# The value products of two head pairs in one group, in every second slot, and the side work in another order

## The reference, cut to what matters

```
x: [16, 512, 128]                      # 16 batches, 512 tokens, 128 channels
x = x + 0.5 * ffn(layernorm(x))        # spiking FFN: relu(x Wfc^T)^2 Wproj^T, 5 steps of a membrane
x = x + attention(layernorm(x))        # 16 heads of 64, ALiBi slope * distance, causal, softmax
x = x + 0.5 * ffn(layernorm(x))        # the same FFN weights

attention(x):
  q, k, v = split(x @ w_qkv);  q *= 64 ** -0.5
  p   = softmax(causal(q k^T - slope_h * |i - j|))
  out = concat_h(p v) @ w_out + b_out
ffn(x): y = relu(x Wfc^T)^2 Wproj^T;  5 times: mem = 0.9 mem + y - (mem > 1);  result = mean of (mem > 1)
```

## Time and profile before

| what | value |
| --- | --- |
| device time, median of 3 runs | 1568.95 us (1568.69 to 1569.36) |
| the profiled execution's own time | 1571.02 us |
| its span in the trace | 1569.2 us |
| granted TensorE clock, mean | 0.998 of full speed |
| busy: PE, PEld | 99%, 80% |
| busy: DVE, ACT, POOL | 70%, 83%, 59% |
| DMA moved | 163.10 MB, mean 104 GB/s |

### The profile page before, as it was taken

The page is one execution under the profiler, slowest core; times in us unless marked ns, Lnnn a source line. Parts: engine busy times, 40 slices in busy tenths (PEclk is TensorE's granted clock), DMA queues, the critical chain, the costliest instruction groups (busy, mean ns, idle before and its releaser), DMA issues.

```text
span 1569.2 us, 33807 instructions
## 1 busy us (share of the span) xinstructions
PE 1547.5 (99%) x10399; PEld 1252.8 (80%) x10399; DVE 1102.2 (70%) x4091; ACT 1301.9 (83%) x3497; POOL 928.3 (59%) x1255
## 2 busy tenths in 40 slices
PE   8999999999999999999999999999999999999998
PEld 7778878887887888888788788878888878888776
DVE  6576776676776677776677766767776777766745
ACT  6888888888887888888888888888888888888884
POOL 4556656666665566556656566666655665566552
PEclk9999999999999999999999999999999999999999
DMA  4454454444455445444444544444554454444540
GB/s 119 91 115 105 98 121 99 105 107 101 107 111 113 98 92 118 108 105 105 104 109 98 121 99 103 107 102 105 111 115 98 94 120 104 102 105 102 114 103 20
DMA packets 80194, 163.10 MB, mean 104 GB/s; under 512 B 12816, under 2 KB 30864, under 8 KB 79888
## 3 DMA queue, kind: packets, MB, share of 16 engines
q1 hardware_dynamic: 80016, 160.94, 47.2%
HBM read 6.88 MB, written 4.19 MB: 7 GB/s over the span
## 4 chain that ended last, share of the span: by engine, by line
PE 96%; DVE 2%; ACT 1%; issue 1%; POOL 0%; POOLq 0%; DVEq 0%
PE bank L497 19%; PE bank L483 18%; PE bank L469 12%; PE bank L470 10%; PE bank L449 8%; PE bank L450 7%; PE bank L453 7%; PE bank L544 7%; PE bank L554 2%; PE bank L555 2%; PE bank L557 2%; PE bank L527 1%; ACT prob L1149 1%; PE bank L646 1%; PE bank L564 0%
## 5 line engine op out<-in xcount | busy, mean ns | idle before, releaser
L1350 POOL TENSOR_TENSOR prob<-prob,rsum 128x512 f32<-128x512 f32 (+3 forms) x1024 | 746.3, 742 | 583.7 <-DVE rsum L805 581.4
L1149 ACT ACTIVATE prob<-negsc,negmax 128x512 f32<-128x512 f32 (+3 forms) x1024 | 576.8, 566 | 164.6 <-DVE negmax L796 162.6
L796 DVE CUSTOM_DVE_ANT_0 negsc<-bank,dist 128x512 f32<-128x512 f32 (+3 forms) x1024 | 467.5, 475 | 0.3 <-issue 0.3
L805 DVE RECIPROCAL rsum<-sums 128x1 f32<-128x1 f32 (+1 forms) x768 | 123.4, 161 | 399.5 <-PE bank L470 382.4
L1162 ACT COPY probT<-bank 128x512 f32<-128x512 f32 x635 | 355.5, 587 | 46.4 <-PE bank L483 40.6
L483 PE MATMUL bank<-ident,prob 128*128 128x128 f32 x2540 | 356.1, 273 | 0.5 <-POOL prob L1350 0.3
L469 PE MATMUL bank<-keys,queries 128*128 128x256 f32 (+2 forms) x1024 | 350.3, 353 | 2.1 <-issue 2.0
L483 PEld LDWEIGHTS bank<-ident,prob 128*128 128x128 f32 x2540 | 299.1, 140 | 28.7 <-POOL prob L1350 5.6
L470 PE MATMUL bank<-keys,queries 128*128 128x256 f32 (+2 forms) x1024 | 319.7, 324 | 0.0
L497 PE MATMUL bank<-probT,vals 128*64 128x512 f32 x2032 | 301.5, 439 | 0.2 <-DVE queries L920 0.2
L497 PEld LDWEIGHTS bank<-probT,vals 128*64 128x64 f32 x2032 | 134.4, 136 | 159.6 <-issue 124.6
(11 more groups left out here) (143 smaller groups left out, 2190.1 us busy)
## 6 DMA issues: line engine op xcount, KB each, us to landing
queries<-queries SPq DMA_DIRECT2D x381, 256.0 KB, 2.9
keys<-k_lo SPq DMA_DIRECT2D x254, 128.0 KB, 2.4
keys<-keys SPq DMA_DIRECT2D x127, 128.0 KB, 2.3
x_in<-in_L_attn_x_dram SPq DMA_DIRECT2D x16, 256.0 KB, 3.1
out_dram<-x SPq DMA_DIRECT2D x15, 256.0 KB, 2.7
prob<-in_L_attn_w_qkv_dram SPq DMA_DIRECT2D x1, 1024.0 KB, 7.4
prob<-in_L_attn_w_qkv_dram SPq DMA_DIRECT2D x1, 512.0 KB, 8.2
probT<-in_L_attn_w_out_dram SPq DMA_DIRECT2D x1, 512.0 KB, 9.4
```

Source lines behind the costliest of these rows:

```text
L796: ins = dve.tensor_tensor_reduce(negsc[:, k % 3, col:col + WIDTH[i]], src, dist[:, N - WIDTH[i]:N], SLOPES[2 * p + h], MASKED, ALU.add, AL ...
L805: dve.reciprocal(rsum[:, p % 2, cols], sums[:, p % 2, cols]).then_inc(s_rsum, 1)
L1149: ins = act.activation(prob[:, p % 2, h, PCOL[i]:PCOL[i] + WIDTH[i]], negsc[:, k % 3, col:col + WIDTH[i]], ACT.Exp, bias=negmax[:, p % 2, ...
L1350: ins = pool.tensor_tensor(pr, pr, rsum[:, p % 2, seg:seg + 1].to_broadcast([P, WIDTH[i]]), ALU.mult)
```

## The change

1. The value products of two pairs stand directly behind one another, in slots 1, 3, 5 and 7, instead of those of one pair in every slot. A pair's value products come two or three slots behind its scores instead of two, so the ring `probT` grows from 10 to 20 places.
2. All tables of the side work and of the order within a beat are others: which beat each "q", "k", "v", "t", "fc", "y", turn, accumulate, membrane step and norm has. `SIDE` has 48 entries as before, of the same kinds. The values' index `i` now runs from 0 to 7 over the batch (`i // 2` is the pair of pairs).
3. In the tail, the statistics of the third norm are aggregated, inverted and used by halves: two tiles, then two tiles, where all four went together.

```diff
-TRING = 10
+TRING = 20
 TBEAT = [
-    [1, 2, 2, 5, 5],
+    [1, 1, 2, 3, 4],
...
-ACCBEAT = [7, 6, 8, 8, 11, 7, 11, 8]
-OUTEV = (2, 1)
+ACCBEAT = [5, 10, 6, 13, 7, 11, 8, 8]
+OUTEV = (2, 3)
...
 SIDE = [
-    (2, 0, "fc1", 3, 1), (2, 0, "q", 0, 0), (2, 1, "ot", 0, -1), (2, 2, "y1", 0, 1), (2, 2, "k", 0, 0),
-    (2, 3, "v", 0, 0), (2, 4, "pv", 0, 0), (2, 5, "y1", 1, 1),
...
+    (2, 0, "q", 0, 0), (2, 0, "fc1", 2, 1), (2, 2, "k", 0, 0), (2, 3, "v", 2, 0), (2, 4, "fc1", 3, 1),
+    (2, 4, "ot", 0, -1),
+    (3, 0, "v", 3, 0), (3, 0, "k", 0, 0), (3, 2, "q", 0, 0), (3, 3, "pv", 0, 0), (3, 3, "pv", 1, 0),
...
-SPIKE3 = [(6, 4), (7, 3), (8, 3), (8, 4), (9, 2), (9, 4)]
-LN1 = dict(stats=(0, 0), aggregate=(0, 2), rstd=(0, 3), normalise=(0, 4))
+SPIKE3 = [(7, 3), (8, 5), (9, 2), (9, 2), (9, 4), (9, 4)]
+LN1 = dict(stats=(0, 0), aggregate=(0, 1), rstd=(0, 2), normalise=(0, 2))
...
+        def pv_pair(b, s, i):
+
+            return before(b, s, 3 - i)
...
+        def acc_at(p):
+
+            return divmod((p - p % 2 + 3) * BEATS + ACCBEAT[p], BEATS)
...
                 elif kind == "pv":
                     for j in PVORDER:
-                        pv(bank or side_bank[n % 2], *before(b, s, 2), j)
+                        pv(bank or side_bank[n % 2], *pv_pair(b, s, i), j)
...
                         if part == "A":
-                            for back in (3, 2):
-                                if ACCBEAT[(s + 2 - back) % PAIRS] == k + BEATS * (back - 2) and exists(*before(b, s, back)):
-                                    accumulate(*before(b, s, back))
+                            for p in range(PAIRS):
+                                if acc_at(p) == (s, k):
+                                    accumulate(b, p)
+                                elif acc_at(p) == (s + PAIRS, k) and b > 0:
+                                    accumulate(b - 1, p)
...
                 for t in range(NT):
+                    if w == 3 and t == NT // 2:
+                        dve.wait_ge(s_rstd[3], B + 1)
...
                         ins = dve.bn_stats(stats[:, 2, t, :], x2[:, t, :])
-                ins.then_inc(s_stats[3], 1)
-                dve.wait_ge(s_stats[3], b + 1)
-                aggregate(3, b)
+                    ins.then_inc(s_stats[3], 1)
+                    dve.wait_ge(s_stats[3], B + half)
+                    for t in range(half * NT // 2, (half + 1) * NT // 2):
+                        ins = dve.bn_aggr(meanvar[:, 2, t, :], stats[:, 2, t, :])
+                    ins.then_inc(s_mv[3], 1)
...
-                bb, pp = before(b, p, 2)
+                bb, pp = before(b, p, TRING // len(TRUNS))
...
-                inverse_std(3, B - 1)
+                for half in range(2):
+                    tiles = TILE_HALVES[half]
+                    pool.wait_ge(s_mv[3], B + half)
+                    pool.tensor_tensor(vareps[:, 2, tiles], meanvar[:, 2, tiles, 1], eps[:, tiles], ALU.add).then_inc(s_ve[3], 1)
+                    pool.wait_ge(s_ve[3], B + half)
+                    pool.tensor_tensor(rstd[:, 2, tiles], vareps[:, 2, tiles], minus_half[:, tiles], ALU.pow).then_inc(s_rstd[3], 1)
```

More of the change, by code:

```diff
@@ L316, in freed @@
             if kind == "pv":
-                bb, pp = before(b, s, 2)
-                return s_attlo, pair_no(bb, pp)
+                return s_attlo, pair_no(*pv_pair(b, s, i))
             return s_x2, b + 1
@@ L324, in last_user @@
                 s, _, kind, i, off = SIDE[m]
-                if m % 2 == n % 2 and off in offsets and (kind != "pv" or exists(*before(b, s, 2))):
+                if m % 2 == n % 2 and off in offsets and (kind != "pv" or pv_exists(b, s, i)):
                     return freed(kind, i, b + off, s)
@@ L609, in slot @@
                             for n, kind, i, off, _ in side_at(s, k, offsets):
-                                if kind == "pv" and not exists(*before(b, s, 2)):
+                                if kind == "pv" and not pv_exists(b, s, i):
                                     continue
@@ L764, in tail @@
                     wait(pe, *last_user(len(SIDE) - (len(SIDE) - n) % 2, b, (-1, 0)))
-                for back in (3,):
-                    if ACCBEAT[PAIRS - 1] >= BEATS:
-                        accumulate(b, PAIRS - 3)
+                for p in range(PAIRS - 2):
+                    if acc_at(p) >= (PAIRS, 0):
+                        accumulate(b, p)
                 for j in PVORDER:
@@ L935, in low_half @@
                 elif kind == "pv":
-                    attention_low((bank or side_bank[n % 2]), *before(b, s, 2))
+                    attention_low((bank or side_bank[n % 2]), *pv_pair(b, s, i))
             def third_spikes(b, s, k):
@@ L1001, in slot @@
                     for n, kind, i, off, ss in side_at(s, k - 1, offsets):
-                        if kind == "pv" and not exists(*before(b, ss, 2)):
+                        if kind == "pv" and not pv_exists(b, ss, i):
                             continue
@@ L1218, in high_half @@
                     act.copy(ysb[:, i * 2 * C:(i + 1) * 2 * C], src[:, 0:2 * C]).then_inc(s_ysb[w], 1)
-                elif kind == "pv" and exists(*before(b, s, 2)):
-                    att_out((bank or side_bank[n % 2]), *before(b, s, 2))
+                elif kind == "pv" and pv_exists(b, s, i):
+                    att_out((bank or side_bank[n % 2]), *pv_pair(b, s, i))
             def slot(b, s, par, offsets):
```

68 lines of the change are left out of this document (35 added, 33 removed), and 21 rows, old and new, of the table SIDE.

## The result

The changed kernel takes 1578.84 us (median of 3 runs, 1576.63 to 1579.60) against 1568.95 before: ratio 1.0061, 95% interval 1.0047 to 1.0075. It is slower by 0.6%, where the forecast was 1549.0 us (1544 to 1557) and faster with 93%. The profiled execution took 1579.60 us with a span of 1577.8.

What follows compares the result with a forecast made beforehand. TensorE's own instruction list was taken as the bound. From the profiled 1571.02 us: -20.8 (twos) + 2 (keys) + 0 (start) - 1.0 (tail) = 1551.2; the median run is 2.07 less, so 1549 us, range 1544 to 1557.

Steps and rivals of the forecast that it cites:

- What bounds the kernel, and a switch's price: TensorE's own instruction list sets the time; entering and leaving a value group costs 0.33 us (0.31 to 0.36).
- The twos save 20.8 us: Value products of two pairs in one group: 63 entries and exits go, at 0.33 us each (19.5 to 22.7).
- Rival D: At the handover inside a doubled group the second pair pays the whole switch again: no gain, 1570 us; 3%.
- C: Rival: a weight load of 0.137 us shows at each handover between pairs, up to 8.6 us: 1558 us; 5%.
- The other tables: Reordered side work and beats: same work, priced at nothing; ScalarE's load was compared with PE's in the light slots.
- rival B: ScalarE sets the pace in light slots 0, 1 and 2, 0.7 us a batch: 1560 us; 8%.
- rival A: The keys come late for slot 3 in every batch, 2.5 us each, 40 us in all: 1587 us; 4%.
- PE's idle time in the loop grows by more than some 5 us: The sign, in the new trace's loop, by which the forecast would be wrong.
- The keys' way, 2 us: Key relay from slot 2's products to slot 3's scores: fits in the median, late landings cost 2 us (0 to 24).
- the margin of 0.3 us: Slot 2's key relay takes 4.8 us against PE's way of 5.1; it fails when a landing is late.
- Start, 0: Batch 0: an earlier first norm against ScalarE's pace in slots 1 and 2; bounds -4 and +3, taken as 0.
- Tail, -1.0: Last batch's third norm by halves: the first FFN products' input ready 1.0 us sooner (0.4 to 1.5).

Runs made afterwards that it cites:

- e13_mid: e10 with one 128-column full-weight product between the two halves of each doubled value group, 63 in all: 1590.79 us, ratio 1.0139.
- e14_ahead: e10 with the same 63 products of 128 columns ahead of the doubled value groups, not within them: 1571.36 us, ratio 1.0015.
- e3: Changed kernel with VectorE's low half of the attention behind a value group before the next scores' bias and maximum: 1574.38 us, ratio 1.0042.
- e6: Changed kernel with one VectorE spike step moved from slot 4, beat 5 to slot 5, beat 1: 1568.71 us, ratio 1.0000.
- e9: e6 with attention low halves ahead of the next scores' maximum behind the value groups of slots 1, 3 and 5 only: 1566.31 us, ratio 0.9983.
- e10: e9 with the first of the two low halves of slot 7's group early too, the second late: 1561.54 us, ratio 0.9954.
- e7: Changed kernel with slot 2's key products ahead of the two accumulations before them, the output turn's copy one beat later: 1589.15 us, ratio 1.0127.
- e12: e10 with e7's edits, and slot 2's query products and third fc1 product exchanged to give the keys another bank: 1570.32 us, ratio 1.0009.
- e5: Changed kernel with VectorE's order as in e3, but the reciprocal of the beat before last ahead of the low half: 1573.73 us, ratio 1.0029.
- e11: Changed kernel with the last batch's third norm done whole again, not by halves: 1578.90 us, ratio 1.0059.
- e2: Changed kernel with the first norm's six VectorE spike steps spread over slots 4 and 5: 1585.72 us, ratio 1.0110.

## Why the prediction was wrong

*What bounds the kernel, and a switch's price: right.* 0.31 to 0.36 us by the earlier trace rows, 0.31 to 0.34 by e13_mid and e14_ahead. *The twos save 20.8 us: right as a term.* The changed kernel has 63 runs of 32 products, no surcharge at the handover. Rival D is out, and so is C: the step at the handover is 0.10 us, less than one load's 0.137. The Trainium skill ("TensorEngine Tiling (Array Packing)", Key Properties) has it that a change of mode drains the engine and a change of the tile alone doesn't; the trace agrees, with nothing at the handover. The Trainium skill ("TensorE: Matmul & The Clock Gate", part 3, "What overlaps and what doesn't") has it that loads overlap with running products only if the row group differs; by the same 0.10 us that does not hold here, within a pair or between two.

*"The other tables. They add and remove no work ... I take nothing": the step that failed.* I asked of the new order only whether ScalarE's load fits (rival B) and whether the keys' relay does (rival A). I did not ask what VectorE's queue has in front of the things that PE and POOL wait for. By the rows and e3, e6, e9 and e10 these were two: the spike steps ahead of the reciprocal that opens slot 5 (e6: 10.1 us), and the maxima ahead of the low half of a group that is now twice as long (e10 against e6: 7.2 us, in slots 0 and 2). With smaller ones they make the 1.66 us a batch, 23 us in batches 1 to 14, against a saving of 18.5. So the term that I put at nothing was 23 us. That VectorE is busy for only 70% hid it: a load says nothing on the order of a queue. I had even set the point to look at ("PE's idle time in the loop grows by more than some 5 us"), but gave it no cause, no price and no chance; no rival was a wait behind VectorE.

*The keys' way, 2 us: right in kind, somewhat low in size.* The mechanism was the margin of 0.3 us, failing when a landing is late. In batch 3, counted from 0:

```profile
340.54 0.46 SPq L399 DMA_DIRECT2D keys<-k_lo  x1
...
344.49 0.47 PE L478 MATMUL bank<-keys,queries 128*128 128x512 f32 x1 [0.70 <-issue]
```

3.95 us from the issue to the scores; this transfer landed after 3.9 us, where the median of its line is 2.3. Such waits came at the head of slot 3 in 6 of 16 batches (3.8 us in all), and some more at its second tile: batches 1 to 14 take 0.30 us more in the mean than the sum of their slots' medians, 4.2 us. But the kernel before has 2.4 us of the same kind in these batches, so the change added 1.8 there; the heads of slot 3 in batches 0 and 15 add 0.3 and 1.2. Rival A (every batch) is out; the two mends tried, e7 and e12, both cost more than they gave.

*Start, 0: wrong by some 3 us.* Batch 0 took 93.13 us after 91.60, with 0.46 us more ahead of it, where three groups should have saved 1.0. I had put ScalarE's pace in slots 1 and 2 against an earlier norm. The wait for the norm did fall, from 3.7 to 1.7 us, but the heads of slots 2 and 5 wait 2.07 and 1.45 us for the queries' transfers, which was no term of mine. Seven traces with the same order on PE in batch 0 (the changed kernel, e3, e5, e6, e9, e10, e11) have these two waits, of 2.1 to 2.5 and 1.4 to 1.5 us, and reach the end of batch 0 at 118.6 to 120.5 us (e2, with its other waits, at 122.3), against 118.1 before less the groups' 1.0. So 1.5 us at least seem to belong to the change; how much of the rest is scatter stays open, with one trace of the kernel before.

*Tail, -1.0: 0.6 to 0.7 by e11.* The inversions of two tiles took 0.70 us, not 0.83, but the second half's statistics began 0.7 us behind the first's end: VectorE makes the first half's aggregate and the second half of `x2` in between.

The sum: 1551.2 forecast for the profiled execution, 1579.60 measured. Of the 28.4 us, batches 1 to 14 hold 22.9 (1338.5 us measured; 1332.1 of before, less 56 x 0.33 = 18.5, plus 2), the start with batch 0 3.0, the last batch with the tail 2.6 (1.2 of it the keys' wait at the head of slot 3).

Which part is shown and which argued: that moving one spike step gives 10.1 us back, that the low halves' place gives 7.2 more, and that a switch costs 0.31 to 0.34 are shown by single edits. What keeps e10 at 94.08 us and not 93.7 (0.17 us at the queries of slot 5, 0.24 in slot 6 behind a low half) is read from the traces; e14_ahead, where the second is gone, bears it out, the first is not tried. e10 is still 10.3 us above the 1551.2 of the forecast: by its trace these two places make 5.8 us over batches 1 to 14, more late landings than forecast 1.1, the start 2.4 and the end 1.1. None of these has a run of its own.

## What to carry to other kernels

Where work on the bounding engine is put into longer runs, first list what the other engines hand back to it in that time, and for each such result what stands ahead of it in its engine's queue: here that, and not the load, decided. Look for the place of a side step of 1 us behind a reciprocal or a bank's last read before one in front, and try it by itself: of the six edits to VectorE's queue here (e2, e3, e5, e6, and e9 and e10 on top of e6) one, e2, cost 6.9 us and five gained 2.4 to 10.1. And when a saving is gone, look for it in the chain and in the slots' durations: the steps between starts give the saving and the waits apart, busy times show neither.

## What the runs showed of the hardware

- Behind a wait, the next step of 512-column products is about 0.1 us longer too: 0.34 us between the starts at 716.42 and 716.76, and at 723.56 and 723.90 in e7_keys, against 0.23 for such steps elsewhere. A start that is 0.27 us late so costs slot 2 its 0.37.
- A change between products with 64-column and 128-column weights costs 0.31 to 0.34 us there and back; a second bank and other values cost nothing.
- A plain fp32 product of 128 columns shows as two records and costs two steps: 0.22 to 0.25 us ahead of each value group (e14_ahead against e10), where single records in a row are 0.11 apart.
- The key transfers, 2.4 us in the median, land after 2.2 to 4.8 us in the changed kernel (line 399): in batch 3 the scores came 3.95 us behind the issue, and in 10 of 16 batches PE did not wait for them at the head of slot 3.
